# A transformer block with top-64 attention on one core: the flag of missed rows, the order of the counts, the norms and the gated products are rearranged

## The chip, the core and the metric

The kernel runs on one core of a Trainium2 chip. The metric is the device time of one execution in microseconds, lower is better. Engines are called by the profile's names: PE (TensorE matmul), PEld (its weight loads), DVE (VectorE), ACT (ScalarE), POOL (GpSimd), SP (SyncE).

## What is computed

For 16 sequences of 512 tokens and width 128, the reference does this (cut to what matters):

```python
x = x + layernorm(attn(layernorm(x)))
x = x + layernorm(ffn(layernorm(x)))

# attn: 16 heads of 64, 16 memory keys in front of the 512 keys
dots = einsum('bhid,bhjd->bhij', q, k) * scale
dots = einsum('bhij,hk->bkij', dots, pre_proj)      # heads mixed
dots = where(causal, neg, dots)
vk   = top_k(dots, 64)[..., -1:]                    # the 64th largest of each row
dots = where(dots < vk, neg, dots)
attn = softmax(dots)
attn = einsum('bhij,hk->bkij', attn, post_proj)     # heads mixed again
out  = einsum('bhij,bhjd->bhid', attn, v)  ->  out @ Wo + bo

# ffn: hidden width 384, weights are int / 127
h = silu(gate) * up ;  down
```

Softmax weights need the 64th largest score of each of 16 x 16 x 512 rows; that search is the bulk of the work of DVE, ACT and POOL.

## The kernel before

**Steps.** The loop over batches holds 16 steps, one for each mixed head, and every step handles all 512 query rows of a head as four row tiles t = 3, 2, 1, 0, of 528, 400, 272 and 144 columns (causal keys plus 16 memory keys). The work is a pipeline over steps: at step g, PE makes the scores of head g, ACT counts for heads g-1, g-2 and g-3, DVE selects for head g-4, exponentials are taken for head g-5 (`LAG_E`), weights are applied for head g-6 (`LAG_P`), and PE multiplies by the values for head g-7 (`LAG_V`). Every engine has its own instruction stream, written out by hand as `step(s)`, and semaphores join them. The first batch (kind "first") and the last (kind "last") lack parts of it, and a "drain" of one more batch ends the pipeline. The FFN of batch b-1 and its norms ride along in steps 7 to 15 of batch b.

**Finding the 64th largest.** Three guesses of a threshold are improved in turn. `count(k)` on ACT runs a Sign activation over each of the four tiles, whose accumulator gives how many scores lie above guess k. From these counts DVE moves the three guesses (`moves`, ten small dependent operations from L1076 to L1102). `count_found` (L1024) marks the scores above the last guess and counts them; POOL subtracts (`hidden`, L1284), DVE takes the 8 largest of what is left (MAX8, L1038), and L1041 and L1046 pick the threshold `kth` among them. `missed` (L1056) says for which rows this window of 8 does not hold the answer.

**The flag of missed rows.** PE sums `missed` over the 128 partitions (L772) into one of the two `misc` PSUM banks, ACT copies the five sums to `flags` in SBUF (L921), and DVE reads the last of them into a register between its second and third MAX8 (`value_load`, L1036). If it is over zero, `general_kth` sorts the tile the long way, behind the branch at L1118. Then DVE applies the threshold (L1127), `rinv` (L1132) gives the reciprocal row sums, and POOL scales the four tiles (L1276).

**Shared PSUM banks.** The two `misc` banks serve all small products in turn: G (query side of the next head's scores), U (value products), XT and X1T (transposes), MEM, PM, GATE, UP, DOWN and FLAG. The table `EXTRAS` says which two of them a step makes beside G. PE makes one, ACT copies it out and adds one to the semaphore `misc_free`; PE makes a product only when the one two places before it has been copied.

**Order within a step before.** ACT: count(2), count(1), the first extra, transposed weights 0, G, FLAG, transposed weights 1, count(0), the second extra, transposed weights 2, four exponentials. PE: scores, first extra, G, weigh, turn 0, turn 1, flag, turn 2, second extra. POOL: small copies, scaling, `hidden`, copy of pmem, and at the end `extras` (layer norms, the residual sums and the product `f_up * f_gate`, L1312). A norm is four POOL operations: the variance plus eps, its power -0.5, and a subtraction (L1196) and a multiplication (L1200) over 128x512.

## Time and profile before

| | |
|---|---|
| time, median of 3 runs | 3606.48 us (3604.53 to 3608.33) |
| profiled execution | 3610.26 us, span 3608.5 us |
| busy share of the span | ACT 88%, DVE 82%, PE 79%, POOL 56% |
| granted TensorE clock, mean | 0.88 |
| batches | 15 periods of about 211 us between step 0 of batch 1 and step 0 of batch 16, where nothing unusual happens |
| HBM traffic | 4 GB/s over the span |

A busy share is an average over the run. Each engine works through its stream in order, so what counts is where an engine waits inside a step and what released it. In the views of waits, the tile on the left belongs to the instruction that waited, and the one on the right to the instruction that ended the wait. "issue" is time in which the engine waited for nothing that the profile shows, its own queue's register and branch work for example.

### The profile page before, as it was taken

To read this page: it belongs to the slowest core of one execution; us is meant where nothing else is said; L and a number is where in the kernel's file an instruction comes from. 1 tells how busy PE (TensorE), PEld (TensorE's weight loads), DVE (VectorE), ACT (ScalarE), POOL (GpSimd) and SP (SyncE) were. 2 spreads that over 40 slices of the span, in tenths; PEclk is the share of its full clock that TensorE was granted. 3 is DMA by queue.
4 is the path that set the end of the run, shared out by engine and by line. 5 is a ranking of instruction groups with operands and counts; after the bars stand their busy time and mean duration, and the time that the engine had idled before them with its cause. 6 is when DMAs were issued, how large, how long until landed. Compare 5 with 4: busy or idle time off the path is not lost. (4 is left out here: it accounts for less than half of the span.)

```text
span 3608.5 us, 70619 instructions
## 1 busy us (share of the span) xinstructions
PE 2833.9 (79%) x13751; PEld 1830.1 (51%) x13751; DVE 2962.0 (82%) x12236; ACT 3177.0 (88%) x9018; POOL 2009.9 (56%) x3687
## 2 busy tenths in 40 slices
PE   7788787878868887788878768877787888777765
PEld 3455555555545555555555545555455555555544
DVE  4588888888888888888888888888888888888883
ACT  1799999999979999999999979998899999999982
POOL 3355655555555565655655545564655555565544
PEclk9888989898988988888998988988898898989876
DMA  1000000000000000000000000000000000000000
GB/s 41 7 2 2 5 8 5 8 2 5 8 4 8 5 2 8 5 8 5 8 2 5 8 4 8 5 8 2 5 8 5 8 5 2 8 5 8 2 7 4
DMA packets 31403, 22.65 MB, mean 6 GB/s; under 512 B 3201, under 2 KB 30338, under 8 KB 30722
## 3 DMA queue, kind: packets, MB, share of 16 engines
q1 hardware_dynamic: 30722, 16.03, 1.6%
q14 instruction: 554, 4.54, 0.4%
q8 instruction: 127, 2.08, 0.2%
HBM read 11.83 MB, written 4.19 MB: 4 GB/s over the span
## 5 line engine op out<-in xcount | busy, mean ns | idle before, releaser
L881 ACT ACTIVATE signs<-scores,state 128x528 int8<-128x528 f32 (+3 forms) x3072 | 1760.0, 573 | 199.5 <-DVE state L1102 106.6
L1276 POOL TENSOR_SCALAR probs<-probs,rinv 128x528 f32<-128x528 f32 (+3 forms) x1024 | 541.4, 549 | 1416.3 <-DVE rinv L1132 1415.3
L747 PE MATMUL t_bank<-ident,probs 128*128 128x128 f32 x2560 | 519.4, 329 | 590.1 <-POOL probs L1276 540.8
L1284 POOL TENSOR_TENSOR work<-scores,work 128x528 f32<-128x528 f32 (+3 forms) x1024 | 887.6, 903 | 15.8 <-DVE work L1024 15.8
L723 PE MATMUL s_bank<-xn,gT 128*128 128x512 f32 (+3 forms) x2048 | 800.0, 515 | 9.5 <-ACT gT L813 6.8
L734 PEld LDWEIGHTS y_bank<-u_all,probsT 128*128 128x128 f32 x5120 | 631.3, 197 | 135.5 <-issue 122.6
L747 PEld LDWEIGHTS t_bank<-ident,probs 128*128 128x128 f32 x2560 | 312.0, 160 | 712.3 <-issue 554.9
L734 PE MATMUL y_bank<-u_all,probsT 128*128 128x128 f32 x5120 | 636.9, 281 | 7.8 <-ACT probsT L892 7.7
L1127 DVE SCALAR_TENSOR_TENSOR probs<-scores,kth,expo 128x528 f32<-128x528 f32 (+3 forms) x1024 | 521.9, 564 | 82.4 <-issue 70.9
L881 ACT ACTIVATION_READ_ACCUMULATOR signs<-scores,state 128x1 f32 x3072 | 573.8, 187 | 0.0
L1024 DVE TENSOR_SCALAR_CACHE_REDUCE work<-scores,state 128x528 f32<-128x528 f32 (+3 forms) x1024 | 527.6, 553 | 46.6 <-DVE state L1102 41.4
L723 PEld LDWEIGHTS s_bank<-xn,gT 128*128 128x128 f32 x2048 | 379.0, 220 | 343.6 <-issue 327.2
L1038 DVE MAX8 state<-work 128x8 f32<-128x528 f32 (+3 forms) x1024 | 463.7, 505 | 74.2 <-ACT flags L813 39.0
L902 ACT ACTIVATE expo<-scores,negmax 128x528 f32<-128x528 f32 (+3 forms) x1024 | 505.4, 571 | 0.0
L1144 DVE TENSOR_SCALAR_CACHE_REDUCE scores<-s_bank,memmax 128x512 f32<-128x512 f32 (+3 forms) x1024 | 501.9, 546 | 3.4 <-PE s_bank L725 3.4
L892 ACT COPY probsT<-t_bank 128x512 f32<-128x512 f32 (+1 forms) x768 | 392.6, 512 | 93.5 <-PE t_bank L747 93.4
L609 PE MATMUL misc<-b_all,xn 128*128 128x512 f32 x512 | 355.0, 782 | 9.0 <-ACT xn L813 4.0
L644 PE MATMUL misc<-xn,a_all 128*128 128x512 f32 x512 | 263.7, 597 | 0.0
L725 PE MATMUL s_bank<-causal,ident 128*128 128x128 bf16 x1024 | 232.1, 227 | 0.0
L725 PEld LDWEIGHTS s_bank<-causal,ident 128*128 128x128 bf16 x1024 | 108.3, 106 | 139.5 <-issue 103.4
L1076 DVE TENSOR_TENSOR state<-counts,consts 128x12 f32<-128x12 f32 x258 | 54.8, 212 | 122.0 <-ACT signs L881 118.0
L813 ACT COPY gT<-misc 128x512 f32<-128x512 f32 x256 | 152.7, 596 | 0.9 <-PE misc L644 0.9
(148 smaller groups left out, 3240.2 us busy)
## 6 DMA issues: line engine op xcount, KB each, us to landing
xwork<-in_L_attn_x_dram SPq DMA_DIRECT2D x17, 256.0 KB, 2.9
xres<-in_L_attn_x_dram SPq DMA_DIRECT2D x16, 256.0 KB, 3.0
out_dram<-ybuf SPq DMA_DIRECT2D x16, 256.0 KB, 2.4
u_all<-in_L_attn_Wq_dram SPq DMA_DIRECT2D x1, 512.0 KB, 3.8
u_all<-in_L_attn_Wk_dram SPq DMA_DIRECT2D x1, 512.0 KB, 4.6
u_all<-in_L_attn_Wv_dram SPq DMA_DIRECT2D x1, 512.0 KB, 5.4
u_all<-in_L_attn_Wo_dram SPq DMA_DIRECT2D x1, 512.0 KB
expo<-in_L_ffn_w_gate_dram SPq DMA_DIRECT2D x1, 192.0 KB, 4.8
```

The costliest lines, as they stand in the source:

```text
L723: nc.tensor.matmul(score_part(t, 0, KEYS[t]), lhsT=gT[s % 2][:, t * P:(t + 1) * P], rhs=xn[par][:, 0:KEYS[t]], start=True, stop=False, ski ...
L734: mm = nc.tensor.matmul(y_bank[:, t * P:(t + 1) * P], lhsT=probsT[:, h % 2, at:at + P], rhs=u_all[:, j, h * D:(h + 1) * D], start=False, s ...
L747: mm = nc.tensor.transpose(t_bank[q % 2][:, at:at + P], probs[:, h % 2, KEY_AT[t] + j * P:KEY_AT[t] + (j + 1) * P], ident[:, :])
L881: nc.scalar.activation(signs[:, k, 0:ROW[t]], row(scores, ring(head_of(s, k + 1), RING), t), ACT.Sign, bias=guesses(s % STATES, k, GUESSES ...
L892: nc.scalar.copy(probsT[:, h % 2, PART_AT[q]:PART_AT[q + 1]], t_bank[q % 2][:, 0:PART_AT[q + 1] - PART_AT[q]]).then_inc(t_taken, 1)
L902: nc.scalar.activation(row(expo, ring(head_of(s, LAG_E), ERING), t), row(scores, ring(head_of(s, LAG_E), RING), t), ACT.Exp, bias=negmax[: ...
L1024: v.tensor_scalar(work[:, s % 2, AT[t]:AT[t] + ROW[t]], row(scores, slot_k, t), guessed[:, t:t + 1], None, ALU.is_ge, ALU.add, accum_out=f ...
L1038: v.max(candidates(past)[:, t, 1:9], work[:, s % 2, AT[t]:AT[t] + ROW[t]]).then_inc(select_step, 1)
L1127: v.scalar_tensor_tensor(out=probs[:, slot_p % 2, AT[t]:AT[t] + ROW[t]], in0=row(scores, slot_p, t), scalar=kth[:, bass.ds(slot_p, 1), t], ...
L1144: v.tensor_scalar(keys(scores, slot, t), score_part(t, 0, KEYS[t]), 1.0, memmax[par][:, t, bass.ds(s, 1)], ALU.mult, ALU.max, accum_out=ro ...
L1276: nc.gpsimd.tensor_scalar(prb, prb, rinv[:, slot_p, t:t + 1], 1.0, ALU.mult, ALU.mult).then_inc(scaled, 1)
L1284: nc.gpsimd.tensor_tensor(wrk, row(scores, slot_k, t), wrk, ALU.subtract).then_inc(hidden, 1)
```

## The change

1. **Flag.** The sum over partitions moves out of the `misc` banks into five free columns of the third score bank (`flag_part`). PE makes it just before the last tile of the scores one step later (`raise_flag`). DVE itself copies it to SBUF, after its guesses have been moved and once all scores of the step are made. The register is read only after `count_found`, straight ahead of the branch. ACT's copy and the FLAG place in the `misc` order are gone. `missed` gets two slots.
2. **Counts.** `count(0)`, over the newest head, is the first thing of ACT's step and no longer stands between the copies. `counts` gets two slots.
3. **PE's and ACT's order.** G is made after `weigh`, the first exponential goes ahead of the third copy of transposed weights, the second extra is copied last. `EXTRAS` is rearranged, the FFN products come one step later. `misc_free` becomes one semaphore for each bank.
4. **Norms.** Each norm's two 128x512 operations become four `tensor_scalar` of 128x128, which subtract and multiply at once. `extras` on POOL stand ahead of the scaling instead of at the end of the step. The norms Y and X1 come one step later on POOL.
5. **Products.** ACT only takes the tanh of a gate; it copies neither gate nor up to SBUF. DVE multiplies (tanh + 1) with the gate in PSUM, then the result with up in PSUM. POOL's product is gone. These two stand between `count_found` and the register read in steps 11 to 13.

```diff
-          2: [("XT",), ("U", 4)],
+          2: [("U", 4), ("XT",)],
...
-          9: [("X1T",), ("GATE", 0)],
-          10: [("UP", 0), ("GATE", 1)],
...
+          9: [("U", 12), ("X1T",)],
+          10: [("U", 13), ("GATE", 0)],
+          11: [("UP", 0), ("GATE", 1)],
+          12: [("UP", 1), ("GATE", 2)],
+          13: [("UP", 2), ("DOWN", 0)],
+          14: [("DOWN", 1), ("U", 14)],
+          15: [("U", 15), None]}
...
+            def raise_flag(s, gp):
+
+                pe.wait_ge(bad_ready, gp + 1)
+                at_least(pe, flag_taken, gp)
+                nc.tensor.matmul(flag_part, lhsT=onesP[:, 0:1], rhs=missed[:, (s - 1) % 2, :], start=True, stop=True,
+                                 skip_group_check=True).then_inc(flag_full, 1)
...
+                    if t == SCORE_ORDER[-1] and lagged(kind, s, LAG_P):
+                        raise_flag(s, g - LAG_P)
...
                         elif use[0] == "GATE":
 
-                            act.wait_ge(silu_ready, HC * (b - 1) + 1)
                             act.wait_ge(misc_full, misc_index(kind, b, use) + 1)
-                            nc.scalar.activation(f_tanh[:, use[1], :], misc[misc_place(kind, par, use)][:, :], ACT.Tanh, scale=0.5)
-                            nc.scalar.copy(f_gate[:, use[1], :], misc[misc_place(kind, par, use)][:, :]).then_inc(misc_free, 1)
+                            nc.scalar.activation(f_tanh[:, use[1], :], misc[misc_place(kind, par, use)][:, :], ACT.Tanh,
+                                                 scale=0.5).then_inc(tanh_ready, 1)
                         elif use[0] == "UP":
-                            take(kind, b, par, use, f_up[:, use[1], :])
+                            pass
...
+                    count(0)
                     count(2)
...
-                    if flagged(kind, s):
-
-                        at_least(act, probs_ready, 4 * (g - LAG_E))
-                        take(kind, b, par, ("FLAG", s), flags[:, :], misc[misc_place(kind, par, ("FLAG", s))][0:1, 0:T + 1])
                     take_turned(1)
-                    count(0)
+                    exponentials(0)
+                    take_turned(2)
+                    for p in range(1, T):
+                        exponentials(p)
                     take_extra(1)
-                    take_turned(2)
-                    for p in range(T):
-                        exponentials(p)
...
+                    if applies:
+                        dve.wait_ge(flag_full, gp + 1)
+                        if kind != "drain":
+                            dve.wait_ge(scores_full, 4 * g + 4)
+                        alone(dve)
+                        v.tensor_copy(flags[:, :], flag_part).then_inc(flag_taken, 1)
...
+                        v.scalar_tensor_tensor(out=f_up[:, c, :], in0=f_tanh[:, c, :], scalar=1.0,
+                                               in1=misc[gate_at][:, :], op0=ALU.add, op1=ALU.mult
+                                               ).then_inc(misc_free[gate_at], 1)
...
+                        v.tensor_tensor(f_up[:, c, :], f_up[:, c, :], misc[up_at][:, :], ALU.mult).then_inc(misc_free[up_at], 1)
+
                     if applies:
+                        dve.wait_ge(flag_taken, gp + 1)
+                        alone(dve)
+                        rows_missed = dve.value_load(flags[0:1, T:T + 1].bitcast(I32), min_val=0, max_val=2 ** 31 - 1)
...
-                nc.gpsimd.tensor_tensor(dst[:, :, :], src[:, :, :], meanvar[:, :, 0:1].to_broadcast([P, T, D]),
-                                        ALU.subtract).then_inc(ln_centred, 1)
-                pool.wait_ge(ln_centred, n + 1)
-                alone(pool)
-                nc.gpsimd.tensor_tensor(dst[:, :, :], dst[:, :, :], rstd[:, :].unsqueeze(2).to_broadcast([P, T, D]),
-                                        ALU.mult).then_inc(ln_out, 1)
+                for t in range(T):
+                    nc.gpsimd.tensor_scalar(dst[:, t, :], src[:, t, :], meanvar[:, t, 0:1], rstd[:, t:t + 1], ALU.subtract,
+                                            ALU.mult).then_inc(ln_out, 1)
```

How the instructions stand, at the two places that matter most. DVE, from the 8 largest to the branch, in a step without FFN work. Before, the register is read between the MAX8:

```order
L1038 MAX state<-work 128x8 [waits hidden]
L1038 MAX state<-work 128x8
L1036 TENSOR_LOAD flags [waits misc_free]
L1036 ISA x2
L1038 MAX state<-work 128x8 x2
L1041 SCALAR_TENSOR_TENSOR offset<-offset,state 128x4x9 [waits select_step,offset_ready]
```

```order
L1102 TENSOR_TENSOR state<-state,move 128x12
L1024 TENSOR_SCALAR work,found<-scores,state 128x528 [waits masked,guess_ready,mem_placed]
L1118 COMPARE_AND_BRANCH [waits kth_ready,scaled,t_full,pmem_ready]
```

In the changed kernel, in a step with FFN work (in the others the rows of L1126 to L1134 are absent, and L1111 and L1113 are one row):

```order
L1106 TENSOR_TENSOR state<-state,move 128x12
L1111 ISA [waits flag_full]
L1113 COPY flags<-s_bank 1x5 [waits scores_full]
L1038 TENSOR_SCALAR work,found<-scores,state 128x528 [waits masked,guess_ready,mem_placed]
L1126 ISA
L1128 SCALAR_TENSOR_TENSOR f_up<-f_tanh,misc 128x512 [waits tanh_ready]
L1131 REGISTER_ALU
L1132 ISA [waits misc_free1]
L1134 TENSOR_TENSOR f_up<-f_up,misc 128x512 [waits misc_full]
L1139 TENSOR_LOAD flags [waits flag_taken]
L1139 ISA x2
L276 REGISTER_ALU
```

The branch, L1145, follows directly. The copy with its wait for PE's scores, and the register read, now stand between the guesses and the branch.

PE, from the transposes of a head's last weights to the scores of the next step. Before:

```order
L747 MATMUL t_bank<-ident,probs 128x128 x3
L770 REGISTER_ALU
L273 REGISTER_ALU [waits bad_ready]
L772 MATMUL misc<-missed,onesP 1x5 [waits misc_free]
L742 REGISTER_ALU
L273 REGISTER_ALU [waits scaled]
L747 MATMUL t_bank<-ident,probs 128x128 [waits t_taken]
L747 MATMUL t_bank<-ident,probs 128x128
L273 REGISTER_ALU
L609 MATMUL misc<-b_all,xn 128x512 [waits misc_free]
L273 ISA [waits misc_free]
L723 MATMUL s_bank<-xn,gT 128x512 [waits masked]
```

Now, the same stretch and the scores behind it (a step whose second extra is absent):

```order
L766 MATMUL t_bank<-ident,probs 128x128 [waits t_taken]
L766 MATMUL t_bank<-ident,probs 128x128
L475 REGISTER_ALU
L276 ISA [waits misc_free0]
L742 MATMUL s_bank<-xn,gT 128x512 [waits masked]
L744 MATMUL s_bank<-causal,ident 128x128
L276 REGISTER_ALU
L742 MATMUL s_bank<-xn,gT 128x384 [waits masked]
L744 MATMUL s_bank<-causal,ident 128x128
L742 MATMUL s_bank<-xn,gT 128x128
L744 MATMUL s_bank<-causal,ident 128x128
L731 MATMUL s_bank<-missed,onesP 1x5 [waits flag_taken,bad_ready,masked]
```

The flag's product has left the transposes and stands in the scores, ahead of their last tile; DVE's copy waits for that tile too.

## Rows read from the trace of the kernel before

**Rows 1.** Head of the page.

```profile
span 3608.5 us, 70619 instructions
```

**Rows 2.** One batch: length; PE, PEld, DVE, ACT, POOL busy; clock.

```profile
1785.69:1997.01 211.32, 169.38 (x845) 109.72 (x845) 180.35 (x758) 197.36 (x563) 123.80 (x229) 0.90 0.02 6
```

**Rows 3.** What ACT waited for in that batch: us, times, longest.

```profile
ACT signs L881 <- DVE state L1102: 6.7, 5, 2.9
ACT probsT L892 <- PE t_bank L747: 2.6, 1, 2.6
```

**Rows 4.** What DVE waited for in that batch.

```profile
DVE state L1076 <- ACT signs L881: 6.1, 10, 0.8
...
DVE state L1038 <- ACT flags L813: 2.3, 1, 2.3
DVE state L1038 <- issue: 2.1, 5, 0.6
DVE f_up L1064 <- POOL f_up L1312: 1.2, 1, 1.2
DVE probs L1127 <- ACT expo L902: 0.6, 1, 0.6
DVE state L1038 <- POOL work L1284: 0.6, 1, 0.6
```

**Rows 5.** Timeline, ACT in step 4 beside DVE in step 5: start, duration, instruction.

```profile
1832.28 1.18 DVE L1038 MAX8 state<-work 128x8 f32<-128x528 f32 x2
1832.58 0.60 ACT L813 COPY gT<-misc 128x512 f32<-128x512 f32 x1
...
1833.06 0.15 ACT L813 COPY flags<-misc 1x5 f32<-1x5 f32 x1
1833.12 0.58 ACT L892 COPY probsT<-t_bank 128x512 f32<-128x512 f32 x1
...
1833.94 0.66 DVE L1038 MAX8 state<-work 128x8 f32<-128x272 f32 x2 [0.48 <-issue]
```

**Rows 6.** Groups by line and shape in that batch.

```profile
L862 ACT COPY f_gate<-misc 128x512 f32<-128x512 f32 x3 | 1.7, 575 | 0.0
...
L1064 DVE SCALAR_TENSOR_TENSOR f_up<-f_tanh,f_up 128x512 f32<-128x512 f32 x3 | 2.1, 691 | 1.2 <-POOL f_up L1312 1.2
```

**Rows 7.** DVE's timeline around the branch, step 5.

```profile
1838.50 0.76 DVE L1024 TENSOR_SCALAR_CACHE_REDUCE work<-scores,state 128x528 f32<-128x528 f32 x1 [0.17 <-DVE state L1102]
...
1839.56 0.77 DVE L1127 SCALAR_TENSOR_TENSOR probs<-scores,kth,expo 128x528 f32<-128x528 f32 x1 [0.29 <-issue]
```

**Rows 8.** Timeline, a norm on POOL beside DVE's guesses; last row: without a norm.

```profile
1798.58 1.04 POOL L1196 TENSOR_TENSOR xwork<-xwork,meanvar 128x512 f32<-128x512 f32 x1
1798.60 1.05 DVE L1094 TENSOR_TENSOR apart<-state 128x24 f32<-128x24 f32 x1
...
1849.42 0.18 DVE L1094 TENSOR_TENSOR apart<-state 128x24 f32<-128x24 f32 x1
```

**Rows 9.** POOL's groups by line and shape in that batch.

```profile
L1276 POOL TENSOR_SCALAR probs<-probs,rinv 128x528 f32<-128x528 f32 x16 | 11.3, 709 | 84.5 <-DVE rinv L1132 84.5
...
L1276 POOL TENSOR_SCALAR probs<-probs,rinv 128x144 f32<-128x144 f32 x16 | 6.2, 390 | 0.0
...
L1312 POOL TENSOR_TENSOR f_up<-f_up,f_gate 128x512 f32<-128x512 f32 x3 | 3.8, 1267 | 0.0
```

**Rows 10.** Timeline, last transposes of step 5, then the scores of step 6.

```profile
1844.82 0.69 PE L747 MATMUL t_bank<-ident,probs 128*128 128x128 f32 x2
1845.40 2.07 PE L723 MATMUL s_bank<-xn,gT 128*128 128x512 f32 x2
...
1849.02 0.22 PE L725 MATMUL s_bank<-causal,ident 128*128 128x128 bf16 x1
```

**Rows 11.** Timeline, first and last row of the scores of step 5.

```profile
1833.33 1.12 PE L723 MATMUL s_bank<-xn,gT 128*128 128x512 f32 x2
...
1835.92 0.22 PE L725 MATMUL s_bank<-causal,ident 128*128 128x128 bf16 x1
```

More of the change, by code:

```diff
@@ L326, in build @@
         state = sb("state", [P, 2 * (STATES - 1) * STATE + PART])
-        counts = sb("counts", [P, GUESSES * T])
+        counts = sb("counts", [P, 2, GUESSES * T])
         between = sb("between", [P, 2, GUESSES * T])
@@ L413, in build @@
         misc_full = sem("misc_full")
-        misc_free = sem("misc_free")
+        misc_free = [sem(f"misc_free{i}") for i in range(2)]
+        tanh_ready = sem("tanh_ready")
         scores_full = sem("scores_full")
@@ L428, in build @@
         hidden = sem("hidden")
+        flag_full = sem("flag_full")
+        flag_taken = sem("flag_taken")
         offset_ready = sem("offset_ready")
@@ L466, in keys, with freed @@
             return tensor[:, bass.ds(slot, 1), KEY_AT[t]:KEY_AT[t] + KEYS[t]].squeeze(1)
+        def freed(engine, kind, b, n):
+            engine.wait_ge(misc_free[n % 2], turns_of_bank(kind, b, n) + 1)
         def mem_parts(flat):
@@ L706, in memory_y @@
             def memory_y(kind, b):
-                pe.wait_ge(misc_free, misc_index(kind, b, ("PM", 1)) + 1)
+                for i in range(2):
+                    freed(pe, kind, b, misc_at(kind, ("PM", i)))
                 for t in range(T):
@@ L981, in memory_maxima @@
             def memory_maxima(kind, b, par):
-                dve.wait_ge(misc_free, misc_index(kind, b, ("MEM", 1)) + 1)
+                for half in range(2):
+                    freed(dve, kind, b, misc_at(kind, ("MEM", half)))
                 at_least(dve, masked, 4 * H * b)
@@ L1055, in step @@
                         dve.wait_ge(select_step, 1)
[L1056 removed]
+                        at_least(dve, flag_full, ge - 1)
+                        alone(dve)
+                        v.scalar_tensor_tensor(out=missed[:, s % 2, 0:T], in0=spread[:, :], scalar=WINDOW ** 2 + 0.5 - AIM ** 2,
                                                in1=active, op0=ALU.is_gt, op1=ALU.mult,
[L1058 to L1065 removed]
+                                               accum_out=missed[:, s % 2, T:T + 1]).then_inc(bad_ready, 1)
                     if moves:
@@ L1150, in step @@
                         norm_stats(kind, b, "x", xwork)
-                    if s == 8 and kind in ("first", "mid"):
+                    if s == 10 and kind in ("first", "mid"):
                         memory_maxima(kind, b, 1 - par)
@@ L1159, in step @@
                         norm_stats(kind, b, "X1", xres)
-                    if s == 15 and kind != "first":
-                        dve.wait_ge(misc_free, misc_index(kind, b, ("DOWN", 1)) + 1)
+                    if s == 14 and kind != "first":
+                        for i in range(2):
+                            freed(dve, kind, b, misc_at(kind, ("DOWN", i)))
                         norm_stats(kind, b, "Z", ybuf)
```

143 lines of the change are left out of this document (61 added, 82 removed).

## The prediction

> **What bounds the kernel now.** I read the busy time of one batch first, then each engine's waits in it, then the timeline of single steps. The span is 3608.5 us [rows 1]; the profiled execution took 3610.26 us, 0.1% above the median of the runs, 3606.48. One batch takes 211.3 us [rows 2]; 15 such periods make nearly the whole run. In one of them ACT waits 9.3 us: 6.7 for the guesses that DVE has just moved, 2.6 for a transpose behind PE's work on y in step 7 [rows 3]. The rest, 202.0 us, is ACT's own work: ACT sets the pace of most steps. DVE is close behind. It waits 6.1 for ACT's counts, 2.3 and 2.1 in the place of the flag's register read, 1.2 for POOL's product and 1.2 in two small ones, 12.9 in all [rows 4]; its own work, with the gaps of its queue, is 198.4 us. The reader should see two engines within 2% of each other, tied by one loop: count(0) stands late in ACT's step, DVE cannot move the guesses before it, and count(2) of the next step waits for them. Neither can run ahead of the other.
>
> **ACT.** Six copies of 512 columns per batch go (three gates, three ups). One takes 575 ns [rows 6], but the next instruction starts 0.48 us after such a copy (1832.58 to 1833.06) [rows 5]: 6 x 0.48 = 2.9 us. The flag's copy of 149 ns holds ACT for 0.06 us (1833.06 to 1833.12) [rows 5]: 16 x 0.06 = 1.0 us. ACT's own work becomes 202.0 - 3.9 = 198.1 us. Moving count(0) to the front costs nothing, since the scores of that head are stored by then, and it gives ACT a full count to do while the guesses are moved. With DVE no slower than now, the 6.7 us of waiting would go. The 2.6 us in step 7 stay: y is still copied by ACT before PE can go on to weights and transposes, and count(0) now lies ahead of that copy [rows 3].
>
> **DVE, what it gains in work.** *Register read.* Now it stands between MAX8 instructions. Where the flag is late, the next MAX8 starts 0.73 us after the flag's copy has ended (1833.21 to 1833.94) [rows 5]; that is the price of wait, read and checks in DVE's queue. After, it stands directly before the branch. There nothing covers it: between `count_found` and the applied threshold DVE is already idle for 0.29 us because the queue's waits and the branch outlast a 0.76 us instruction [rows 7]. So I add nearly all of it, 0.70 x 16 = 11.2 us. Bounds: 0, if the queue could run ahead of the count after all, and 0.73 x 16 = 11.7. *Flag copy.* Five elements; a gap of 0.17 us for the completion of L1102 is there already [rows 7] and hides part; I take 0.10 x 16 = 1.6 us, between 0 and 0.25 each (0.15 for ACT's same copy [rows 5] and a wait). *Products.* The first stays one instruction of 0.69 us; a second of about the length of a 512-column copy, 0.6 us [rows 6], comes with two waits and its predecessor's completion: 0.85 x 3 = 2.6 us, between 0.6 and 1.1 each.
>
> **DVE, what it sheds.** A DVE operation with two SBUF inputs stands still while POOL runs one of its two-input operations: L1094 takes 1.05 us beside L1196, and 0.18 otherwise [rows 8]. Four norms per batch with two such operations, at about 0.8 each, are 6.4 us; three products of 1.27 us on POOL [rows 9], at about 0.5, are 1.5. After, the products are gone from POOL, and a norm is four pieces. Drawn through 390 ns for 144 and 709 ns for 528 columns [rows 9], a piece of 128 columns takes 0.38 us. If each holds DVE for half its length, that is 4 x 4 x 0.19 = 3.0 us per batch. The relief is 6.4 + 1.5 - 3.0 = 4.9; 0.9 more for the residual sums, which then fall beside `count_found`, an operation with one input: 5.8 us, between 2 and 8.9.
>
> The rows do not show a POOL operation of the form of the new pieces beside DVE's guesses. By the Trainium skill, page "SBUF — State Buffer", section "Who interferes with whom", a VectorE instruction with two SBUF inputs contends with any GpSimd instruction that reads SBUF, and whoever starts first holds the port to its end. The trace agrees for the form that it shows (1.05 us against 0.18). By that rule the pieces hold DVE too, as assumed; without it the relief would be 8.8 and the time some 45 us less. By the same page the new products, each with one input in PSUM, cannot be held at all.
>
> **The sum.** DVE's own work becomes 198.4 + 11.2 + 1.6 + 2.6 - 5.8 = 208.0 us per batch, against 198.1 of ACT. So the engine that sets the pace changes. DVE may now lag behind ACT by a few microseconds and catch up in steps without norm statistics, but not fully: its flag copy waits for all scores of the step. From the applied threshold (1839.56) to the last transposes (1844.82) are 5.26 us, from there to the scores 0.58 [rows 7, 10]; scores 2.8 [rows 11]; in most steps a second extra, about 1.1 (as the 512-column scores [rows 11]); the flag's product, copy, count, read and branch 0.2 + 0.3 + 1.06 + 0.7. That loop is 12.0 us, against 208.0 / 16 = 13.0 on average, but light steps of DVE are near 12. At the low clock level (the first pair of scores 2.07 us instead of 1.12 [rows 10, 11]) it is 13.0 and costs something in light steps. With the stall of step 7 I add 0.7 us. A batch takes 208.7 instead of 211.3: 15 x 2.6 = 39 us. The end of the run, where the last FFN goes alone through three gates and two norms, gives about 3 us more. 3606.5 - 42 = **3565 us**.
>
> **The rivals.**
>
> *ACT keeps the pace (0.18).* If the read is covered, or POOL's norms cost DVE nothing, DVE needs 196 to 200 us and ACT's 198.1 + 2.6 in step 7 is the period: 10.6 x 15 = 159 us less, about 3450. For it: the removed 6.7 us of waiting is real, and of the batch's 16 register reads only six show a gap now [rows 4]. Against: the 0.29 us of idle time before the branch.
>
> *PE's loop decides, and the kernel gets slower (0.22).* Place: DVE's wait for the last scores ahead of its flag copy. Each microsecond by which the loop of 12.0 us outgrows DVE's step is lost whole, since the next threshold starts it again. It decides from about 13.2 us on (211.3 / 16). A low-clock stretch gives 13.0; with 1 us more for the copy of transposed weights 0, which now stands behind three counts on ACT, it is 14. Should that hold in ten of 16 steps, a batch is 211.3 + 4 = 215 and the time 3665. For it: ACT reaches that copy one full count later in its step, and PE's last transposes wait for it. Against: at full clock the loop has 1 us of room.
>
> *Gains and losses cancel (0.09).* Two microseconds per batch more than summed: 3600 to 3613.
>
> *The forecast's case (0.51)*: DVE's own work sets the pace, 3510 to 3599.
>
> **Chances and range.** Within 0.2%, 3599 to 3614, is about what a measurement of this kernel cannot tell from no change. Faster: 0.51 + 0.18 = 0.69, plus 0.01 of the third rival; same 0.08; slower 0.22. The range leaves out the far half of the ACT rival below and of the PE rival above: 3465 to 3640.
>
> **What the changed profile would show.** ACT's wait for DVE's guesses moves from count(2) to steps 0, 1, 8, 9 and 11 to 15 and grows to about 8 us per batch; DVE's waits for ACT's counts (6.1) vanish. The idle time before the applied threshold grows from 0.29 to about 1.0 us in every step: if it stays near 0.3, the term of 11.2 is wrong and the first rival holds. L1094's successor, L1098, stays below 0.6 us beside a norm. If the flag's copy shows waits for PE's scores in most steps, the second rival holds. The forecast fails if the period of a batch isn't DVE's own work within 2 us.

## The result: 3652.64 us instead of 3606.57, 1.3% slower

The changed kernel takes 3652.64 us (median of 4 runs, 3646.99 to 3656.0); the kernel before, run beside it, takes 3606.57 (3604.53 to 3608.33). The ratio is 1.0126, with a 95% interval of 1.0109 to 1.0144. The forecast was 3565 us. The profiled execution took 3646.99 us, the fastest of the four; that of the kernel before took 3610.26, more than any of its runs here. So the two traces lie 36.7 us apart and not 46.

Head and instruction line of the page of the changed kernel, to be held against [rows 1]:

```profile
span 3645.2 us, 70387 instructions
```

One batch of the changed kernel, read as [rows 2] (length; PE, PEld, DVE, ACT and POOL busy; clock). DVE is busy 2.0 us less than before and ACT 2.5, and yet the batch is 1.7 us longer. The clock is 0.90 in both.

```profile
1802.58:2015.59 213.01, 168.20 (x848) 110.34 (x847) 178.34 (x777) 194.84 (x541) 125.67 (x235) 0.90 0.02 6
```

Not all batches are like this one. I measured from the applied threshold of step 0 to the next such threshold, 15 times in each trace. The mean is 213.8 us before and 216.0 after. Three of the 15 take 220 to 228 us before and 223 to 231 after, so the 15 periods of "about 211 us" hide something: in four steps of the run, three in these periods and one behind them, the flag is over zero, and DVE sorts a tile the long way. This row shows it for the changed kernel, 8 MAX8 in each of four sorts (duration in ns: shortest, median, longest; then first and last start in us); the kernel before also has 32 (L1001).

```profile
L1015 DVE MAX8 top<-probs x32: 310/711/711, 1021.6 to 3550.6; 128x8 f32<-128x528 f32 x24, 128x8 f32<-128x144 f32 x8
```

The sorts are in both kernels and so don't explain the difference. The batch shown has none.

What DVE waited for in that batch, against [rows 4]. The waits for ACT's counts (6.1) and for the late flag (2.3 and 2.1) are gone. In their place stand idle time before the applied threshold (16.1 us, 4.5 before), 1.0 us in each of the 16 steps, for which the profile shows no other engine, and a wait for PE's last scores.

```profile
DVE probs L1154 <- issue: 16.1, 16, 1.2
DVE flags L1113 <- PE s_bank L744: 2.8, 3, 1.6
DVE f_up L1134 <- DVE f_up L1128: 0.6, 3, 0.2
```

What ACT waited for, against [rows 3]. It waits 13.3 us instead of 9.3: the engine that set the pace before now waits for others. The wait isn't at the guesses but at the transposed weights, which stand at the end of a chain that DVE starts: applied threshold, row sums, POOL's scaling, PE's transposes.

```profile
ACT probsT L908 <- PE t_bank L766: 12.2, 9, 3.4
ACT signs L897 <- DVE state L1106: 1.1, 2, 0.6
```

DVE's timeline in a step without FFN work. Against [rows 7], L1038 (L1024 before) to L1154 (L1127 before) is 1.75 us instead of 1.06. `missed` starts 0.29 us after `spread`, where it was 0.20 us before, and the copy of the flag stands between L1106 and L1038, which are 0.45 us apart instead of 0.34. The next such threshold starts at 1873.12, 12.44 us after this one, and not one of DVE's idle times in between is a wait for another engine.

```profile
1856.11 0.16 DVE L1062 SCALAR_TENSOR_TENSOR spread<-found 128x4 f32<-128x4 f32 x1
1856.40 0.17 DVE L1067 SCALAR_TENSOR_TENSOR missed<-spread,consts 128x4 f32<-128x4 f32 x1
...
1858.48 0.17 DVE L1106 TENSOR_TENSOR state<-state,move 128x12 f32<-128x12 f32 x1
1858.69 0.15 DVE L1113 COPY flags<-s_bank 1x5 f32<-1x5 f32 x1
1858.93 0.76 DVE L1038 TENSOR_SCALAR_CACHE_REDUCE work<-scores,state 128x528 f32<-128x528 f32 x1
...
1860.68 0.77 DVE L1154 SCALAR_TENSOR_TENSOR probs<-scores,kth,expo 128x528 f32<-128x528 f32 x1 [0.98 <-issue]
...
1873.12 0.77 DVE L1154 SCALAR_TENSOR_TENSOR probs<-scores,kth,expo 128x528 f32<-128x528 f32 x1 [0.98 <-issue]
```

The timeline at the end of step 7, three engines. ACT copies y only behind two counts; PE had waited 2.99 us for it, and needs until 1893 for bias, weights and G before it can transpose. ACT waits 3.44 us for the transposes, and the scores come so late that DVE waits 1.63 us at its flag copy in step 8.

```profile
1886.59 0.56 ACT L929 COPY ybuf<-y_bank 128x512 f32<-128x512 f32 x1
...
1887.21 1.12 PE L623 MATMUL y_bank<-bias,ones 1*128 1x512 f32 x2 [2.99 <-ACT ybuf L929]
1888.26 3.83 PE L753 MATMUL y_bank<-u_all,probsT 128*128 128x128 f32 x20
...
1893.73 0.58 ACT L908 COPY probsT<-t_bank 128x512 f32<-128x512 f32 x1 [3.44 <-PE t_bank L766]
...
1898.59 0.15 DVE L1113 COPY flags<-s_bank 1x5 f32<-1x5 f32 x1 [1.63 <-PE s_bank L744]
```

A step with products: from `count_found` (1938.53) to the applied threshold are 3.29 us instead of 1.75. The register read isn't hidden by them; the idle time ahead of L1154 is the same 1.0 us.

```profile
1938.53 0.76 DVE L1038 TENSOR_SCALAR_CACHE_REDUCE work<-scores,state 128x528 f32<-128x528 f32 x1
...
1939.21 0.68 DVE L1128 SCALAR_TENSOR_TENSOR f_up<-f_tanh,misc 128x512 f32<-128x512 f32 x1
...
1940.10 0.69 DVE L1134 TENSOR_TENSOR f_up<-f_up,misc 128x512 f32<-128x512 f32 x1 [0.21 <-DVE f_up L1128]
1941.82 0.77 DVE L1154 SCALAR_TENSOR_TENSOR probs<-scores,kth,expo 128x528 f32<-128x528 f32 x1 [1.03 <-issue]
```

### The profile page after: what moved, and what is told of

Read it like the earlier page. It is cut to its first block and busy times, and to the rows that moved or that the text cites. A ratio compares the mean times of both kernels' runs of the same rounds, so it can differ in the third digit from the quotient of the medians.

```text
span 3645.2 us, 70387 instructions
## 1 busy us (share of the span) xinstructions
PE 2805.3 (77%) x13751; PEld 1832.9 (50%) x13751; DVE 2939.2 (81%) x12540; ACT 3139.1 (86%) x8666; POOL 2034.0 (56%) x3767
## 5 line engine op out<-in xcount | busy, mean ns | idle before, releaser
L1309 POOL TENSOR_TENSOR work<-scores,work 128x528 f32<-128x528 f32 (+3 forms) x1024 | 887.8, 899 | 13.1 <-DVE work L1038 13.1
L766 PEld LDWEIGHTS t_bank<-ident,probs 128*128 128x128 f32 x2560 | 348.9, 173 | 1025.6 <-issue 854.2
L742 PE MATMUL s_bank<-xn,gT 128*128 128x512 f32 (+3 forms) x2048 | 814.4, 509 | 6.2 <-ACT gT L828 4.0
L1154 DVE SCALAR_TENSOR_TENSOR probs<-scores,kth,expo 128x528 f32<-128x528 f32 (+3 forms) x1024 | 534.2, 577 | 258.9 <-issue 256.1
L1038 DVE TENSOR_SCALAR_CACHE_REDUCE work<-scores,state 128x528 f32<-128x528 f32 (+3 forms) x1024 | 527.4, 553 | 26.2 <-issue 2.9
L918 ACT ACTIVATE expo<-scores,negmax 128x528 f32<-128x528 f32 (+3 forms) x1024 | 542.0, 590 | 0.0
L742 PEld LDWEIGHTS s_bank<-xn,gT 128*128 128x128 f32 x2048 | 366.9, 215 | 310.8 <-issue 275.7
L1047 DVE MAX8 state<-work 128x8 f32<-128x528 f32 (+3 forms) x1024 | 443.8, 500 | 0.0
L618 PE MATMUL misc<-b_all,xn 128*128 128x512 f32 x512 | 315.2, 702 | 7.6 <-ACT u_all L828 7.6
L828 ACT COPY u_all<-misc 128x512 f32<-128x512 f32 x256 | 147.1, 575 | 8.1 <-PE misc L618 8.1
```

The source lines that it names most:

```text
L742: nc.tensor.matmul(score_part(t, 0, KEYS[t]), lhsT=gT[s % 2][:, t * P:(t + 1) * P], rhs=xn[par][:, 0:KEYS[t]], start=True, stop=False, ski ...
L766: mm = nc.tensor.transpose(t_bank[q % 2][:, at:at + P], probs[:, h % 2, KEY_AT[t] + j * P:KEY_AT[t] + (j + 1) * P], ident[:, :])
L918: nc.scalar.activation(row(expo, ring(head_of(s, LAG_E), ERING), t), row(scores, ring(head_of(s, LAG_E), RING), t), ACT.Exp, bias=negmax[: ...
L1038: v.tensor_scalar(work[:, s % 2, AT[t]:AT[t] + ROW[t]], row(scores, slot_k, t), guessed[:, t:t + 1], None, ALU.is_ge, ALU.add, accum_out=f ...
L1047: v.max(candidates(past)[:, t, 1:9], work[:, s % 2, AT[t]:AT[t] + ROW[t]]).then_inc(select_step, 1)
L1154: v.scalar_tensor_tensor(out=probs[:, slot_p % 2, AT[t]:AT[t] + ROW[t]], in0=row(scores, slot_p, t), scalar=kth[:, bass.ds(slot_p, 1), t], ...
```

## Experiments

The theory to be tested: DVE sets the pace, and its queue has become longer by the register read ahead of the branch and by more small things than were summed. The rivals: the chain through PE's scores sets the pace, or ACT's new order costs the time. Each ratio is to the kernel before, run on the same chip. "Changed kernel" is 3652.64 us, measured on yet another occasion: the kernel before took 3606.57 beside it and 3605.57 to 3608.73 beside the experiments, and the runs of one kernel lie 3 to 12 us apart. A difference in us between two kernels can therefore be off by a few us.

### The register read

**A second read.** To the changed kernel a second, unused register read is added behind the first. It has its range checks, but no wait of its own.

```diff
                         rows_missed = dve.value_load(flags[0:1, T:T + 1].bitcast(I32), min_val=0, max_val=2 ** 31 - 1)
+                        dve.value_load(flags[0:1, 0:1].bitcast(I32), min_val=0, max_val=2 ** 31 - 1)
```

> The changed kernel with a second register read behind the first, whose value is not used. A dose test of the read's place. Theory A: the read lies on DVE's path with nothing beside it, so 0.6 to 0.7 us in each of 256 steps, 150 to 180 us more: 3800 to 3830. If the read is covered or DVE has slack: under 40 us more.

Measured 3820.44 us (3819.81 to 3822.82), ratio 1.0598 (1.058 to 1.0615): 168 us more, 0.66 us for each of 256 steps. The idle time before the applied threshold shows it, 1.58 us instead of 0.98:

```profile
1903.75 0.76 DVE L1038 TENSOR_SCALAR_CACHE_REDUCE work<-scores,state 128x528 f32<-128x528 f32 x1
...
1906.10 0.77 DVE L1155 SCALAR_TENSOR_TENSOR probs<-scores,kth,expo 128x528 f32<-128x528 f32 x1 [1.58 <-issue]
```

So DVE's queue is on the path in nearly every step, and a read there is lost whole.

**The flag earlier, the read where it is.** PE sums the flag of the head that was just checked, in the same step; DVE copies it behind the scores of the step, so that it waits for nothing there.

```diff
-                nc.tensor.matmul(flag_part, lhsT=onesP[:, 0:1], rhs=missed[:, (s - 1) % 2, :], start=True, stop=True,
+                nc.tensor.matmul(flag_part, lhsT=onesP[:, 0:1], rhs=missed[:, s % 2, :], start=True, stop=True,
...
-                        raise_flag(s, g - LAG_P)
+                        raise_flag(s, g - LAG_E)
...
-                    if applies:
-                        dve.wait_ge(flag_full, gp + 1)
-                        if kind != "drain":
-                            dve.wait_ge(scores_full, 4 * g + 4)
-                        alone(dve)
-                        v.tensor_copy(flags[:, :], flag_part).then_inc(flag_taken, 1)
...
+                    if checks:
+                        dve.wait_ge(flag_full, ge + 1)
+                        alone(dve)
+                        v.tensor_copy(flags[:, :], flag_part).then_inc(flag_taken, 1)
```

> The changed kernel, with the flag of a head raised one step earlier (in the scores of step g for head g-5) and copied by DVE at the end of its step, after the last scores have been stored. The register is still read directly ahead of the branch. So only the copy leaves the path between guesses and threshold, and with it its wait for PE's last scores. Theory A, DVE's own serial work sets the pace: it saves the 2.6 us of waits per batch and about 0.15 us per step of copy, 5 us per batch, some 75 us in all: 3575. Theory B, the loop through PE's scores sets the pace, and the trace shows only a part of it: DVE then falls to its work without any of it, 3500 or less.

Measured 3587.51 us (3585.52 to 3589.45), ratio 0.9948 (0.9931 to 0.9964). 65 us go with the flag's earlier product and its copy's new place, 12 us short of the first expectation. The idle time ahead of the applied threshold is still 0.98 us in a plain step; in the batch from 1770.93 to 1982.29 DVE has no wait for scores any more (2.8 us above, 42 us over 15 batches). Two other waits of 1.5 us have come, for an exponential and for a product of PE. The copy has left the way between guesses and branch:

```profile
1801.35 0.17 DVE L1106 TENSOR_TENSOR state<-state,move 128x12 f32<-128x12 f32 x1
1801.74 0.76 DVE L1038 TENSOR_SCALAR_CACHE_REDUCE work<-scores,state 128x528 f32<-128x528 f32 x1 [0.23 <-DVE state L1106]
```

**The flag earlier, the read between the MAX8.** As before it, with the read moved to between the second and third MAX8.

```diff
-                        for t in ORDER:
+                        for p, t in enumerate(ORDER):
+                            if p == 2:
+                                dve.wait_ge(flag_taken, gp + 1)
+                                alone(dve)
+                                rows_missed = dve.value_load(flags[0:1, T:T + 1].bitcast(I32), min_val=0,
+                                                             max_val=2 ** 31 - 1)
...
-                        dve.wait_ge(flag_taken, gp + 1)
-                        alone(dve)
-                        rows_missed = dve.value_load(flags[0:1, T:T + 1].bitcast(I32), min_val=0, max_val=2 ** 31 - 1)
```

> As the one with the early flag, and the register is read between the second and the third MAX8 again, as in the kernel before; the flag has been there since the step before. Theory A: 0.70 us less in each of 256 steps of DVE, 180 us of DVE time against the early flag alone; DVE then needs about 200 us per batch and ACT (198 us and its wait in step 7) becomes the limit, so some 90 to 110 us less than the early flag alone, 3465 to 3500. Theory B, or a read that was covered all along: no difference to the early flag alone beyond 10 us.

Measured 3513.33 us (3511.0 to 3518.41), ratio 0.9747 (0.973 to 0.9763), another 74 us, 13 us above the expected range. Its timeline shows the read gone from the path: four MAX8 take 1.72 us with the read among them (in the changed kernel 1.74 without it), and 0.28 us are left before the applied threshold.

```profile
1760.55 0.76 DVE L1038 TENSOR_SCALAR_CACHE_REDUCE work<-scores,state 128x528 f32<-128x528 f32 x1 [0.23 <-DVE state L1111]
...
1761.60 0.77 DVE L1150 SCALAR_TENSOR_TENSOR probs<-scores,kth,expo 128x528 f32<-128x528 f32 x1 [0.28 <-issue]
...
1766.96 1.72 DVE L1052 MAX8 state<-work 128x8 f32<-128x528 f32 x4
```

The gain is less than 168 us because another engine is reached on the way down. In a batch of 204.81 us ACT still waits 6.1 us, and DVE now waits 7.5 us for ACT and PE; with DVE's queue shorter, ACT's own work of about 199 us is next.

### The order of the counts

**The counts alone, in the kernel before.** `count(0)` first and `counts` with two slots; flag, norms and products as before.

```diff
+                    count(0)
                     count(2)
...
-                    count(0)
```

> The kernel before with one part of the change alone: count(0) stands first in ACT's step, counts have two slots. Theory A: the loop of count(0), guesses and count(2) held both engines; without it ACT's 6.7 us of waits and DVE's 6.1 us per batch go and ACT's own 202 us plus its wait in step 7 is the period, about 205: 100 us less, 3505. Rival: the copies of transposed weights now stand behind three counts, PE and the flag's register read get them 2.6 us later, and the gain is given back there: 3560 or more.

Measured 3784.71 us (3779.17 to 3789.6), ratio 1.0491 (1.0473 to 1.0509): 178 us more. It lies on the rival's side ("3560 or more"), but neither expectation foresaw the size. What DVE and ACT waited for in one batch (1870.06 to 2094.50):

```profile
DVE state L1038 <- ACT flags L813: 27.0, 11, 3.9
...
ACT u_all L813 <- PE misc L609: 10.5, 8, 1.7
ACT f_tanh L861 <- PE misc L703: 4.9, 3, 1.6
```

The flag still goes through a shared PSUM bank and ACT's copy. With three counts in front, ACT frees the banks late, and DVE waits 27.0 us at the read (2.3 in [rows 4]). With the flag on its old path the new order of the counts costs 178 us; whether it gains anything in the changed kernel itself, nothing here tests. Parts of the change that were priced one by one are tied together.

**The count late again.** In the kernel with the early flag and the read between the MAX8, `count(0)` goes back behind the second copy of transposed weights.

```diff
-                    count(0)
                     count(2)
...
                     take_turned(1)
+                    count(0)
```

> The version with the early flag and the read between the MAX8 (3513 us), with count(0) back behind the second copy of transposed weights. Tests what the counts' order is worth once DVE is not the limit. Theory: count(0) late closes the loop of counts and guesses again, 5 to 7 us of ACT's waits per batch come back, 75 to 105 us more: 3590 to 3620. Rival: the order of counts gives nothing, and the gain comes from the copies that ACT no longer makes: 3513 within 15 us.

Measured 3554.45 us (3552.36 to 3557.09), ratio 0.9849 (0.9832 to 0.9865): 41 us more than 3513.33 (37 by the two ratios), between the two expectations. DVE's wait for the counts is back, larger than in [rows 4], so the order is worth about 40 us once the flag is out of the way:

```profile
DVE state L1085 <- ACT signs L897: 8.4, 11, 2.3
```

### The norms

**Norms in two operations.** The changed kernel with the old pair of 128x512 operations (subtract, multiply) in the norms' new place.

```diff
-                for t in range(T):
-                    nc.gpsimd.tensor_scalar(dst[:, t, :], src[:, t, :], meanvar[:, t, 0:1], rstd[:, t:t + 1], ALU.subtract,
-                                            ALU.mult).then_inc(ln_out, 1)
+                nc.gpsimd.tensor_tensor(dst[:, :, :], src[:, :, :], meanvar[:, :, 0:1].to_broadcast([P, T, D]),
+                                        ALU.subtract).then_inc(ln_centred, 1)
...
+                nc.gpsimd.tensor_tensor(dst[:, :, :], dst[:, :, :], rstd[:, :].unsqueeze(2).to_broadcast([P, T, D]),
+                                        ALU.mult).then_inc(ln_out, 4)
```

> The changed kernel with each norm as a subtraction and a multiplication over 128x512 again, in the new place ahead of the scaling. Tests the term for POOL's norms holding up DVE. If the form matters as the prediction had it (6.4 us per batch for the two operations, 3.0 for the four pieces), 3.4 us per batch more: 3700. Rival, the new place alone gives the relief, since the norm's operations then fall beside DVE's one-input operations and the branch: under 15 us more.

Measured 3670.97 us (3661.46 to 3673.25), ratio 1.0162 (1.0145 to 1.0179): 18 us more, 13 by the two ratios. The old form costs DVE something in the new place too, but less than half of what the theory asked for and nearer to the rival; the rest of the relief comes from the place. In the timeline a norm's first operation starts 0.69 us after DVE's L1099 has begun, and so meets no long row of two-input operations as it did in [rows 8]. It still meets one, L1107, which takes 0.95 us; L1106 of the changed kernel, the same operation, takes 0.17 in the rows above:

```profile
1824.45 0.18 DVE L1099 TENSOR_TENSOR apart<-state 128x24 f32<-128x24 f32 x1
...
1825.14 1.04 POOL L1224 TENSOR_TENSOR xwork<-xwork,meanvar 128x512 f32<-128x512 f32 x1
1825.26 0.95 DVE L1107 TENSOR_TENSOR state<-state,move 128x12 f32<-128x12 f32 x1
...
1826.33 1.04 POOL L1228 TENSOR_TENSOR xwork<-xwork,rstd 128x512 f32<-128x512 f32 x1
```

### What else makes the changed kernel slow

**No wait ahead of the sum.** The changed kernel guards the second slot of `missed` by a wait for PE. It is always fulfilled: DVE has waited for that product one step earlier, at the copy of the flag.

```diff
-                        at_least(dve, flag_full, ge - 1)
-                        alone(dve)
                         v.scalar_tensor_tensor(out=missed[:, s % 2, 0:T], ...
```

> The changed kernel, with only the wait for the flag's product and the empty instruction that carries it taken out ahead of the sum `missed` (DVE has already waited for that product one step earlier, so nothing new becomes possible but speed). Theory A, DVE's own queue paces nearly every step: the gap ahead of `missed` shrinks from 0.30 to 0.20 us as before the change, 0.10 x 256 = 26 us less, 3620 to 3632 us. Theory B, the loop through PE's scores or ACT paces the steps: under 8 us less, 3645 to 3653 us.

Measured 3626.33 us (3621.21 to 3629.72), ratio 1.0053 (1.0036 to 1.0069): 26 us less. It starts 0.20 us after `spread` again:

```profile
1857.01 0.16 DVE L1062 SCALAR_TENSOR_TENSOR spread<-found 128x4 f32<-128x4 f32 x1
1857.21 0.16 DVE L1065 SCALAR_TENSOR_TENSOR missed<-spread,consts 128x4 f32<-128x4 f32 x1
```

A tenth of a microsecond of DVE's queue comes back from nearly every step. It is the whole of what theory A asked for. That holds only if DVE's own work is the pace there; the chain through PE's scores and ACT don't change by this edit.

**y sooner.** The changed kernel, with ACT's copy of y ahead of `count(2)`.

```diff
                     count(0)
-                    count(2)
                     if s == LAG_V and kind != "first":
                         ...
                         nc.scalar.copy(ybuf[:, :, :], y_bank[:, :].rearrange("p (t d) -> p t d", t=T)).then_inc(y_taken, 1)
+                    count(2)
```

> The changed kernel, with ACT's copy of y in step 7 between count(0) and count(2) instead of behind count(2). Theory A, the stall of step 7 is lost whole by every engine: about 2.3 us per batch less as in the kernel with the early flag, 3610 to 3625 us. Theory B, DVE's own work sets the period over a batch and it only stands idle there for what it would make up later: under 10 us less, 3643 to 3653 us.

Measured 3628.17 us (3627.72 to 3631.07), ratio 1.0059 (1.0042 to 1.0076): 24 us less. That is between the two expectations and nearer to theory A, the stall that is lost whole. In a batch of 212.76 us DVE's waits for the scores fall from 2.8 to 2.0 us and ACT's for the transposes from 12.2 to 9.6.

**Products later.** The changed kernel, with the block of the two products moved, as it is, from ahead of the register read to behind `rinv`.

```diff
-                    if 11 <= s < 11 + HC and kind != "first":
-                        ...
...
                         v.reciprocal(rinv[:, slot_p % 2, :], rowsum[:, :]).then_inc(rinv_ready, 1)

+                    if 11 <= s < 11 + HC and kind != "first":
+                        ...
```

> The changed kernel, with DVE's two products of steps 11 to 13 behind the reciprocal row sums instead of ahead of the register read. DVE's work is the same. Theory A, in those steps DVE's own work is the pace: under 8 us less, 3645 to 3653 us. Theory B, the loop from the applied threshold over POOL's scaling, PE's transposes and scores back to DVE, or ACT that waits for the transposes, is the pace there: up to 1.6 us x 3 x 15 = 72 us less, about 3610 us with half of it.

Measured 3639.83 us (3635.39 to 3642.3), ratio 1.0089 (1.0073 to 1.0106): 13 us less, between the two expectations and nearer to "DVE's own work is the pace". It is hardly more than the spread of the runs. Of 1.5 us by which the threshold comes sooner in those steps, 0.3 are gained.

**Both.**

> The changed kernel, with both edits: the copy of y sooner and the products late. If DVE's own work is the pace (theory A of the products, theory B of y), 3635 to 3650 us. If the stalls of step 7 and of the product steps are lost whole, the two gains add up: 3575 to 3595 us. The flag path is unchanged in this kernel, so whatever stands above 3439 us here, the time with the flag moved as well, is the price of the flag's new place and of its read straight ahead of the branch.

Measured 3612.4 us (median of 10 runs, 3611.02 to 3616.73), ratio 1.0017 (1.0008 to 1.0027): 40 us less, the sum of 24 and 13 within the spread. The expectation asked for 3575 to 3595 if both stalls were lost whole, and for 3635 to 3650 if neither counted; it is between. With them alone the change comes out 0.2% above the kernel before.

### A version faster than both kernels

The kernel with the early flag and the read between the MAX8, with the same two edits one after the other.

> The version of 3513 us, with ACT's copy of y in step 7 after count(0) instead of after count(2). ACT waits 4.6 us per batch in step 7 for the transposes that stand behind y on PE. If the copy's place is the cause, PE starts 2.6 us sooner and the wait shrinks by about as much: 2.6 x 16 = 40 us less, 3475. If something else holds PE there (memory keys of the head before, POOL), no difference beyond 10 us.

Measured 3478.09 us (3473.34 to 3483.53), ratio 0.9642 (0.9626 to 0.9658): 35 us less than 3513.33, as expected.

> The same, and the two products of steps 11 to 13 on DVE stand behind rinv instead of ahead of the branch. In the version of 3513 us ACT waits 3.1 us per batch in steps 11 to 13 for transposes, which wait for rinv through POOL, and DVE waits 2.4 us for the gate and up that the products read. If their place is the cause, some 2 to 4 us per batch less than the one with the sooner copy: 30 to 60 us, 3415 to 3445. Rival: PE's next G waits for the bank that the products free and the transposes behind G come as late as before: no difference beyond 10 us.

Measured 3439.06 us (3433.84 to 3441.61), ratio 0.9524 (0.9509 to 0.954): another 39 us, in the expected range. The same edit gave 13 us in the changed kernel, where ACT doesn't set the pace. One batch of it, its length 200.79 us, and ACT's one wait of weight:

```profile
1701.73:1902.52 200.79, 161.44 (x848) 105.77 (x847) 176.67 (x778) 193.99 (x541) 126.53 (x235) 0.92 0.02 6
```

```profile
ACT probsT L908 <- PE t_bank L766: 1.5, 1, 1.5
...
ACT ybuf L928 <- PE y_bank L722: 0.2, 1, 0.2
```

ACT waits 1.7 us in a batch and works for the other 199.1: it is the pace again, at the forecast's 198.1 within 1 us. The only difference between this kernel and the one with both edits above is the flag's place and the register read: 3612.4 - 3439.06 = 173 us, 0.68 us for each of 256 steps. This is what the two bring together, not the price of the read: here ACT stops the gain. DVE itself is spared more, in the batches looked at 13 us of idle time ahead of the applied threshold (16.0 against 2.9) and 2.1 us of waits for scores.

## Why the prediction was wrong

**The engine was right, its work too small, and the margin thin.** The prediction set DVE's own work at 208.0 us per batch, and the period at 208.7 against 211.3 before. In the batch shown, DVE's own work is 213.0 - 2.8 = 210.2 us and the period 213.0. So 2.2 us of the miss are work and 2.1 are waits for scores (2.8 where 0.7 were allowed). The forecast lived on a difference of 2.6; a miss of 4.3 turned its sign. By the prediction's own sign of failure, a period more than 2 us away from DVE's own work, it failed too: they are 2.8 apart.

**ACT's part held.** Its own work was forecast at 198.1; it is 213.0 - 13.3 = 199.7 here. It has its slack, as forecast, but spends it at another place: at the transposed weights (12.2 us) rather than at the guesses (1.1 us). The prediction had the wait for the guesses leave count(2) and grow to about 8 us in steps 0, 1, 8, 9 and 11 to 15; that sign was wrong. With a full count ahead of it, count(2) finds its guesses ready, and ACT meets DVE's lateness at the other end of the chain.

**Register read: right.** 11.2 us per batch were added; the idle time before the applied threshold grew from 4.5 to 16.1, by 11.6. The second read costs 0.66 us a step where 0.70 was taken.

**Flag copy, products: right.** L1106 to L1038 is 0.11 us longer in a step, 1.8 us per batch where 1.6 were taken. Products: 3.29 - 1.75 = 1.54 us, less 0.61 for the one instruction before, 0.93 each where 0.85 was taken.

**POOL's relief: right in size by luck.** I added, in both traces, by how much each DVE operation that overlaps one of POOL is longer than the shortest of its form: 11.9 us per batch before, 6.7 after, so 5.2 of relief where 5.8 were forecast. But the pieces of 128 columns were to hold DVE for 3.0 us; they hold it for 0.11. What still holds it is `hidden` (L1309, 3.5), the subtraction of ranks (L1290, 1.5) and the small copy ahead of it (L1284, 0.8). The prediction has them in no term and gives no reason; before, the same three cost about 3.0 us (L1284, L1266, L1260), so they grew by about 3. That growth and the 3.0 us taken for the pieces, which didn't come, cancel. By the run with two operations, 13 to 18 us of the whole run's relief are due to the form and the rest to the place.

**The steps that failed.** Three terms of the sum, all in DVE's part, each tested by taking it away:
- The diff's wait ahead of `missed` (`flag_full`, with an empty instruction) was in no term at all. Taken out, it gives back 26 us. That is more than half of the 46 us by which the kernel became slower.
- "With the stall of step 7 I add 0.7 us": the stall was seen, and ACT's copy of y behind `count(0)` was named, but 0.7 us was too small for the loop that starves DVE in step 8. Moving the copy gives 24 us, 1.6 per batch, and doesn't even remove all of it.
- The place of the products, between `count_found` and the applied threshold, was priced as work only. Moved behind the row sums at the same work, they give 13 us in the changed kernel.

A fourth is small: the end of the run was to be 3 us shorter. In the traces what lies ahead of the 15 periods and behind them is 4.8 us longer; the cause is open.

Together the three give 26 + 24 + 13 = 63 us, if they add up; 24 and 13 did, the first was not run with them. 0.4, 0.2 and 0.2 us per batch too little for read, copy and products and 0.6 too much for relief would be 21 more, 84 in all. That this is near the 88 between 3565 and 3652.64 proves little. The traces divide the 88 otherwise: the mean batch is 2.1 us longer where 2.6 shorter were forecast, 71 us in 15 batches; the ends make 8; and 9 are in no trace, because the two profiled executions lie closer together than the medians. So 84 us of single terms stand against 71 in the batches. The single terms overlap, or the differences between runs carry errors of that size; which, isn't shown. The new order of PE's work wasn't tried by itself.

**The rivals.** "PE's loop decides" ended on the right side, at 3665, but not by its mechanism: it wanted DVE's wait for the last scores in ten of 16 steps, and there are 3 in the batch shown, of 1.63 us in step 8, 0.69 in step 12 and 0.44 in step 14. The 26 us that the removed wait gives back exclude it as the pace of most steps. "ACT keeps the pace" is excluded by the 1.0 us ahead of the branch and by the second read, which is paid in full. It came true in another kernel: with the read hidden and the stalls gone the time is 3439, beside the 3450 that this rival gave.

## What to carry to other kernels

When a change moves the pace to another engine, go through that engine's instruction stream line by line in the diff and price every added wait, empty instruction and register read, even a wait that is always fulfilled: at 256 passes a tenth of a microsecond was 26 us, and the gain forecast was 42. A register read ahead of the branch had nothing to hide behind here; placed between long operations of the same queue, with its value made one step earlier, it cost nothing that the trace shows. Price a stall at the engine that pays for it at the end of the chain, not at the one where it is first seen, and don't price parts of a change one by one where they share a buffer: the counts alone in the kernel before cost 178 us.

## What the runs showed of the hardware

- A register read in DVE's queue with its range checks costs 0.66 us when it stands ahead of a branch, and nothing visible between MAX8 operations (1.72 us for four with it, 1.74 without).
- An already fulfilled wait with an empty instruction costs DVE 0.10 us between two small operations (0.29 against 0.20 us from start to start).
- A piece of 128x128 on POOL, subtract and multiply by two values per partition at once, takes 0.79 us in the median of all 256, where a line through the scaling's sizes gave 0.38. The four pieces of a norm take 3.8 us on average in the batch shown, because some are held up (below). Two operations of 128x512 take 1.04 each. The change makes the norm slower on POOL, and easier for DVE:

```profile
L1224 POOL TENSOR_SCALAR xwork<-xwork,meanvar,rstd 128x128 f32<-128x128 f32 x4 | 4.1, 1026 | 0.2 <-POOL rstd L1220 0.2
```

```profile
L1224 POOL TENSOR_SCALAR ybuf<-ybuf,meanvar,rstd x128: 780/790/1664, 387.2 to 3640.2; 128x128 f32<-128x128 f32 x128
```

- Beside these pieces, DVE's L1154 over 528 columns, which has two SBUF inputs, is hardly ever held; mostly the piece is. In the first rows below, the four pieces in one row and then the fourth by itself, L1154 begins 0.13 us ahead of the fourth piece. L1154 takes its usual 0.77 us and the piece 1.70. In the next it meets POOL's sum of two inputs, L1230, which began 0.47 us earlier, and takes 1.37 us.

```profile
1808.30 4.07 POOL L1224 TENSOR_SCALAR xwork<-xwork,meanvar,rstd 128x128 f32<-128x128 f32 x4 [0.18 <-POOL rstd L1220]
...
1810.54 0.77 DVE L1154 SCALAR_TENSOR_TENSOR probs<-scores,kth,expo 128x528 f32<-128x528 f32 x1 [0.98 <-issue]
...
1810.67 1.70 POOL L1224 TENSOR_SCALAR xwork<-xwork,meanvar,rstd 128x128 f32<-128x128 f32 x1
...
1900.11 1.27 POOL L1230 TENSOR_TENSOR xres<-xres,ybuf 128x512 f32<-128x512 f32 x1
1900.58 1.37 DVE L1154 SCALAR_TENSOR_TENSOR probs<-scores,kth,expo 128x528 f32<-128x528 f32 x1 [0.98 <-issue]
```

  A piece does hold L1154 when it has begun just before. In the rows below the piece began 0.08 us earlier, and L1154 takes 0.92 us.

```profile
3205.21 0.79 POOL L1224 TENSOR_SCALAR ybuf<-ybuf,meanvar,rstd 128x128 f32<-128x128 f32 x1
...
3205.29 0.92 DVE L1154 SCALAR_TENSOR_TENSOR probs<-scores,kth,expo 128x528 f32<-128x528 f32 x1 [0.98 <-issue]
```

  The whole trace of the changed kernel has three cases. In five overlaps the piece began 0.08 to 0.18 us ahead, and L1154 took 0.82 to 0.92 us: as if it could start only 0.23 us after the piece had (0.228 to 0.235 in the five). Where the piece began 0.26 us or more ahead, L1154 took 0.77 to 0.79. Where L1154 began first, or at most 0.01 us behind the piece, the piece waited for the row of L1154 and took 1.33 to 1.70 us, 40 times.

  The Trainium skill, page "SBUF — State Buffer", section "Who interferes with whom", has a VectorE instruction with two SBUF inputs contend with any GpSimd instruction that reads SBUF. The trace agrees for L1230 and for L1224 alike: what differs is how much of the piece's time can hold DVE, 0.23 us of 0.79, and which of the two has begun first. By the rule the prediction took 3.0 us per batch for the pieces. DVE loses 0.11; where the two meet it is mostly POOL that waits, and POOL isn't the pace. The prediction's "holds the port to its end" is also more than the trace shows for a piece, whose hold is over 0.23 us after its start. Which property of the piece makes its hold so short, its one tensor input or the operands per partition, wasn't tried.
